# Two stacks of local attention: `weigh` with its operands exchanged, probabilities divided before it, four PSUM banks in one ring, and new orders on all engines

## The reference, cut to what matters

```python
qkv = x @ Wqkv                       # 128 -> 3 x 1024
q = l2norm(q) * qs;  k = l2norm(k) * ksc
q, k = rotary(q), rotary(k)          # per position, with a scale
sim = einsum('bhwie,bhwje->bhwij', bq, bk2) * 8      # 32 queries, 64 keys
attn = softmax(where(mask, -max, sim), -1)
out = einsum('bhwij,bhwje->bhwie', attn, bv2)
x = out @ Wo                         # 1024 -> 128, tokens shifted
hg = layernorm(x) @ W1 + b1          # 128 -> 2 x 341
x = (a * gelu(gate)) @ W2 + b2
```

## Time and profile before

| | us |
|---|---|
| median of 3 runs | 4099.03 (4097.41 to 4099.03) |
| the profiled execution | 4101.54 |
| its span, first to last instruction | 4099.7 |
| PE busy | 3777.4 (92%) |
| DVE busy | 3244.2 (79%) |
| ACT busy | 2461.2 (60%) |
| POOL busy | 2262.3 (55%) |
| from one group's first PE batch to the next one's (731.10 to 800.17) | 69.07 |

### The profile page before, as it was taken

How to read it: one execution, slowest core, us unless ns; L and a number is a source line. 1 busy time by engine, 2 the same in 40 slices (tenths; PEclk the granted TensorE clock), 3 DMA queues, 4 the chain that set the end, 5 groups by cost and what they waited for, 6 DMA issues and landing times. The chain is left out here.

```text
span 4099.7 us, 159711 instructions
## 1 busy us (share of the span) xinstructions
PE 3777.4 (92%) x63216; PEld 2414.3 (59%) x63216; DVE 3244.2 (79%) x11559; ACT 2461.2 (60%) x4393; POOL 2262.3 (55%) x2174
## 2 busy tenths in 40 slices
PE   4689999999999999997699779999999999999997
PEld 2356666666666666663265446666666666666664
DVE  3478888887888888884699778888888788888884
ACT  1257676766767676763522146767676666667674
POOL 1166666666666666662200056666666666666662
PEclk8699999999999999997799789999999999999998
DMA  1032232332322322220000032232232332322221
GB/s 37 27 77 68 74 83 65 78 79 62 78 76 65 87 67 71 71 65 26 0 1 0 6 84 73 65 78 75 72 83 65 79 79 64 79 77 64 76 64 39
DMA packets 170579, 254.11 MB, mean 62 GB/s; under 512 B 36577, under 2 KB 67681, under 8 KB 169697
## 3 DMA queue, kind: packets, MB, share of 16 engines
q1 hardware_dynamic: 169824, 243.74, 23.2%
HBM read 38.08 MB, written 1.05 MB: 10 GB/s over the span
## 5 line engine op out<-in xcount | busy, mean ns | idle before, releaser
L506 PE MATMUL stack_proj<-stack_w_qkv,stack_xs 128*128 128x512 f32 x2304 | 1190.6, 612 | 72.0 <-POOL stack_xs L1137 44.9
L1145 POOL TENSOR_TENSOR stack_roped<-stack_rot_c,stack_rot_s 128x512 f32<-128x512 f32 x768 | 973.7, 1276 | 350.7 <-DVE stack_rot_s L968 350.6
L1155 POOL TENSOR_TENSOR stack_roped<-stack_roped,stack_rnorm 128x512 f32<-128x512 f32 x768 | 813.3, 1070 | 198.7 <-DVE stack_rnorm L1000 198.7
L1163 POOL TENSOR_TENSOR stack_s_m<-stack_s_m,stack_smax 128x512 f32<-128x512 f32 x384 | 402.5, 1048 | 593.7 <-DVE stack_smax L1011 593.6
L966 DVE TENSOR_TENSOR stack_rot_c<-stack_proj,rot_tables 128x512 f32<-128x512 f32 x768 | 527.8, 687 | 229.5 <-PE stack_proj L506 223.7
L1011 DVE CUSTOM_DVE_ANT_0 stack_s_m<-stack_bank_s,band 128x64 f32<-128x64 f32 x3072 | 476.0, 220 | 156.3 <-PE stack_bank_s L529 149.1
L506 PEld LDWEIGHTS stack_proj<-stack_w_qkv,stack_xs 128*128 128x128 f32 x2304 | 369.0, 192 | 307.8 <-issue 138.8
L977 DVE TENSOR_REDUCE stack_ssq<-stack_sq 128x8 f32<-128x512 f32 x768 | 520.5, 678 | 17.5 <-issue 3.5
L805 ACT ACTIVATE stack_sq<-stack_proj 128x512 f32<-128x512 f32 x768 | 460.9, 600 | 109.2 <-DVE stack_rot_s L968 108.5
L968 DVE TENSOR_TENSOR stack_rot_s<-stack_proj,rot_tables 128x512 f32<-128x512 f32 x768 | 521.7, 679 | 0.0
L514 PEld LDWEIGHTS stack_turn<-ident,stack_roped 128*128 128x128 f32 x3072 | 362.6, 141 | 223.9 <-issue 204.0
(11 more groups left out here) (261 smaller groups left out, 5297.1 us busy)
## 6 DMA issues: line engine op xcount, KB each, us to landing
stack_v_w<-stack_v_nat SPq DMA_DIRECT2D x1152, 130.0 KB
stack_v_w<-stack_v_nat SPq DMA_DIRECT2D x768, 65.0 KB
stack_w_qkv<-table_ffn_qkv SPq DMA_DIRECT2D x192, 96.0 KB, 2.4
stack_w_o<-table_ffn_wo SPq DMA_DIRECT2D x12, 512.0 KB, 3.9
stack_w<-table_ffn_w SPq DMA_DIRECT2D x12, 384.0 KB, 3.3
stack_w<-table_ffn_w SPq DMA_DIRECT2D x12, 192.0 KB, 2.9
x_outer<-L_attn_a_X SPq DMA_DIRECT2D x4, 256.0 KB, 3.6
ret_xpos<-table_xpos SPq DMA_DIRECT2D x1, 1024.0 KB, 5.4
```

The lines of the kernel that those rows point to most:

```text
L506: pe.matmul(bank[:, :], xs[:, T, :], w_qkv[:, g.half, col:col + 512], start=True, stop=True).then_inc(done["proj_" + c], 1)
L1145: pool.tensor_tensor(roped[:, i, T % 2, :], rot_c[:, i % 2, :], rot_s[:, i % 2, :], ALU.add).then_inc(done["roped_" + c], 1)
L1155: pool.tensor_tensor(r, r, rnorm[:, T % 2, i, :].unsqueeze(2).broadcast_to([P, 8, HD]), ALU.mult).then_inc(done["united_" + c], 1)
```

## The change

1. `weigh` is turned round: the values (64 rows by 64 columns) are the loaded operand, the probabilities (32 columns) move. It yields the heads transposed, in `bank_o`, from which `heads_out` copies them. `turn_heads` and `norm_heads` are gone, and so is the column of ones, so that the rows that the spread moves are 2,048 instead of 2,080 bytes.
2. The probabilities are divided before that: `sum_probs` and `invert` on DVE, `scale_probs` on POOL, between `exponent` and `turn_probs`.
3. `proj` and `turnb` become one list `work` of four banks, used in turn by everything; `BANK` gives the first index and the row is added to it.
4. New orders on PE, ACT, DVE and POOL. The values are copied at lag 2 instead of 1, the attention after `scores` is at lag 3 instead of 2, `heads_out` half 1 and `mid` at lag 4; `center` moves from T0 of lag 2 to T3 of lag 1. T2 and T3 of PE, cut below, are as T1 but for the MLP: in T2 gate 2 stands where gate 0 is, lin 1 where gate 1 is, nothing where lin 0 is, and lin 2 behind v1; in T3 `center` stands where gate 0 is, `down` between k0 and v1, nothing else of the MLP.
5. SP's waits name `weighed1` and `proj_v1` alone; what it issues, and behind which tile, is unchanged (layer_loads).

```diff
-        proj = [ps("proj0"), ps("proj1")]
-        turnb = [ps("turn0"), ps("turn1")]
+        work = [ps(f"work{n}") for n in range(4)]
...
                     return
-                wait(pe, f"exped{j}", t)
...
                 if not live(t):
                     return
                 wait(pe, f"pt_set{j}", t)
-                if j == 0:
+                if j == FIRST_PV:
                     pe.wait_ge(v_in[T % 2], (2 * g.number + (tile0 // 2 + T // 2 + 1)) * 160)
                 apart(pe, t)
-                for m in range(4):
-                    for gp in range(2):
-                        for n in range(4):
-                            last = pe.matmul(bank_o[WINDOW * n:WINDOW * (n + 1), gp, m * (HD + 1):(m + 1) * (HD + 1)],
-                                             p_t[64 * gp:64 * gp + 64, j, m, WINDOW * n:WINDOW * (n + 1)],
-                                             v_w[64 * gp:64 * gp + 64, T % 2, n, 2 * m + j, :], start=True, stop=True)
+                for half in range(2):
+                    for n in range(4):
+                        for odd in range(2):
+                            for gp in range(2):
+                                m, at = 2 * half + odd, P * half + WINDOW * n
+                                last = pe.matmul(bank_o[HD * odd:HD * (odd + 1), gp, at:at + WINDOW],
+                                                 v_w[64 * gp:64 * gp + 64, T % 2, n, 2 * m + j, :],
+                                                 p_t[64 * gp:64 * gp + 64, j, m, WINDOW * n:WINDOW * (n + 1)],
+                                                 start=True, stop=True)
                 last.then_inc(done[f"weighed{j}"], 1)
-
-            def turn_heads(t, T, g, j, bank):
-                if not live(t):
-                    return
-                wait(pe, f"normed{j}", t)
-                for n in range(4):
-                    last = pe.transpose(bank[:, P * n:P * (n + 1)], o_n[:, j, n // 2, 2 * (n % 2):2 * (n % 2) + 2, :],
-                                        ident[:, :])
-                last.then_inc(done[f"pe_ot{j}"], 1)
...
             def slot(N, T, G, at, of):
+                row = of(0).row
                 if T == 0:
-                    wait(pe, "squared_q1", N - 1)
-                    center(of(2), proj[0])
-                    wait(pe, "v_out0", N - 1)
-                    project_out(*at(3), proj[1])
-                    wait(pe, "ot_set1", N - 3)
-                    variance(of(2), turnb[0])
-                    wait_group(pe, "center_set", G - 2)
-                    project(*at(1), "v1", proj[0])
+                    wait(pe, "kept_q0", N - 2)
+                    project(*at(1), "k1", work[(0 + row) % 4])
                     wait(pe, "kept_k1", N - 2)
-                    turn_probs(*at(2), 0, turnb[1])
-                    wait(pe, "mid_set", N - 3)
-                    project(*at(0), "k0", proj[1])
-                    wait(pe, "v_out1", N - 1)
-                    project(*at(0), "q0", proj[0])
+                    project(*at(2), "v0", work[(1 + row) % 4])
+                    wait(pe, "mid_set", N - 4)
+                    turn(*at(2), "q1", work[(2 + row) % 4])
+                    wait(pe, "kept_k0", N - 2)
+                    project(*at(0), "q0", work[(3 + row) % 4])
+                    wait(pe, "masked1", N - 3)
+                    scores(*at(2), 0)
+                    wait(pe, "squared_k1", N - 1)
+                    turn_probs(*at(3), 0, work[(0 + row) % 4])
+                    scores(*at(2), 1)
+                    wait(pe, "ot_set1", N - 4)
+                    weigh(*at(3), 0)
+                    wait(pe, "v_out0", N - 2)
+                    turn_probs(*at(3), 1, work[(1 + row) % 4])
+                    wait(pe, "kept_q1", N - 2)
+                    project(*at(0), "k0", work[(2 + row) % 4])
+                    wait(pe, "squared_q0", N - 0)
+                    variance(of(2), work[(3 + row) % 4])
+                    wait(pe, "pt_set0", N - 3)
+                    project(*at(2), "v1", work[(0 + row) % 4])
+                    wait(pe, "ot_set0", N - 3)
+                    weigh(*at(3), 1)
+                    wait(pe, "pt_set1", N - 3)
+                    project(*at(0), "q1", work[(1 + row) % 4])
+                    wait(pe, "squared_k0", N - 0)
+                    turn(*at(1), "q0", work[(2 + row) % 4])
                     wait_group(pe, "std_read", G - 2)
-                    turn(*at(1), "k0", turnb[0])
-                    wait(pe, "normed1", N - 3)
-                    weigh(*at(2), 0)
-                    wait(pe, "pt_set0", N - 2)
-                    turn_probs(*at(2), 1, turnb[1])
-                    wait(pe, "kept_k0", N - 1)
-                    turn(*at(1), "q0", turnb[0])
+                    turn(*at(1), "k1", work[(3 + row) % 4])
+                    wait(pe, "v_out1", N - 2)
+                    project_out(*at(3), work[(0 + row) % 4])
+                    wait(pe, "squared_q1", N - 0)
+                    turn(*at(1), "k0", work[(1 + row) % 4])
+                elif T == 1:
...
+                    turn_probs(*at(3), 0, work[(2 + row) % 4])
+                    wait(pe, "v_out0", N - 2)
+                    up(of(2), "gate", 0, work[(3 + row) % 4])
+                    scores(*at(2), 1)
+                    wait(pe, "ot_set1", N - 4)
+                    weigh(*at(3), 0)
+                    wait(pe, "kept_q1", N - 2)
+                    turn_probs(*at(3), 1, work[(0 + row) % 4])
+                    wait(pe, "squared_q0", N - 0)
+                    project(*at(0), "k0", work[(1 + row) % 4])
+                    wait(pe, "pt_set0", N - 3)
+                    up(of(2), "gate", 1, work[(2 + row) % 4])
+                    wait_group(pe, "gelu0", G - 2)
+                    up(of(2), "lin", 0, work[(3 + row) % 4])
+                    wait(pe, "pt_set1", N - 3)
+                    project(*at(2), "v1", work[(0 + row) % 4])
+                    wait(pe, "ot_set0", N - 3)
+                    weigh(*at(3), 1)
...
             def heads_out(t, T, g, j):
                 if not live(t):
                     return
-                wait(act, f"pe_ot{j}", t)
+                wait(act, f"weighed{j}", t)
                 wait(act, "pe_wo", t - 2)
-                act.copy(o_t[:, T % 2, 4 * j:4 * j + 4, :],
-                         turnb[PROJ[f"ot{j}"][T]][:, :].rearrange("p (g n) -> p g n", g=4)
+                act.copy(o_t[:, T % 2, 4 * j:4 * j + 4, :].rearrange("p (g h) n -> p g h n", g=2),
+                         bank_o[:, :, 0:2 * P].rearrange("p g (h n) -> p g h n", h=2)
                          ).then_inc(done[f"ot_set{j}"], 1)
...
             def slot(N, T, G, at, of):
-                heads_out(*at(3), 1)
-                values_out(*at(1), 0)
-                if T == 0:
-                    center_square(of(2))
-                if T == 1 and live_group(G - 2):
-                    act.preload_act_table_set(TABLE)
+                heads_out(*at(4), 1)
                 if T == 2 and live_group(G - 2):
                     act.preload_act_table_set(TABLE)
+                if T == 3 and live_group(G - 2):
+                    act.preload_act_table_set(TABLE)
+                exponent(*at(3), 0)
+                square(*at(1), "q1")
+                keep(*at(2), "q0")
+                keep(*at(2), "k1")
+                keep(*at(2), "k0")
+                exponent(*at(3), 1)
+                if T == 1:
+                    gain_bias(of(2))
+                square(*at(1), "k1")
+                values_out(*at(2), 0)
+                keep(*at(2), "q1")
+                probs_out(*at(3), 0)
                 guess(*at(1))
-                if T == 0:
-                    center_out(of(2))
-                exponent(*at(2), 0)
+                square(*at(0), "q0")
+                if T == 3:
+                    center_square(of(1))
+                if T == 2:
+                    gelu(of(2), 2)
+                if T == 3:
+                    center_out(of(1))
+                if T == 1:
+                    gelu(of(2), 0)
+                probs_out(*at(3), 1)
+                heads_out(*at(3), 0)
                 if T == 0:
                     inv_std(of(2))
-                values_out(*at(1), 1)
-                probs_out(*at(2), 0)
-                exponent(*at(2), 1)
-                keep(*at(1), "k0")
-                if T == 0:
-                    gain_bias(of(2))
                 square(*at(0), "k0")
-                probs_out(*at(2), 1)
-                square(*at(0), "q0")
-                keep(*at(1), "q0")
-                heads_out(*at(2), 0)
-                square(*at(0), "k1")
-                if T == 0:
+                if T == 1:
                     gelu(of(2), 1)
-                keep(*at(1), "q1")
-                if T == 1:
-                    gelu(of(2), 2)
-                keep(*at(1), "k1")
-                square(*at(0), "q1")
-                if T == 0:
-                    gelu(of(2), 0)
```

(90 more changed lines are left out.)

346 lines of the change are left out of this document (149 added, 197 removed), and 2 rows, old and new, of the table NAMES.

## The result

| us | before | after |
|---|---|---|
| median of the runs | 4099.03 | 4369.65 (4357.48 to 4374.49, 4 runs) |
| the profiled execution, its span | 4101.54, 4099.7 | 4370.48, 4368.7 |
| mean of 44 groups, two stacks | 69.3 | 75.4 |

The change makes the kernel slower: ratio 1.0657, 95% interval 1.063 to 1.0684. The forecast was 4323 us in a range of 4110 to 4460. A fourth execution of the kernel before took 4227.10 us in a slower state, and the median leaves it out.

The account below looks back on a forecast made before the run. TensorE (PE) was taken to bound the kernel before. 4101.5 + 77 (values' loop) + 85 (late w_o) + 47 (late MLP weights) + 15 (clock) = 4325.5, median 2.5 lower: 4323 us, range 4110 to 4460.

Parts of the forecast that it names:

- 1 to 3: On PE, heads' turning gone (-3.8 us a group), `weigh` turned round (+1.9), a drain saved (-0.5): 64.5, 66.5 with waits.
- 2, `weigh`: On PE, the 64-column load sets the pace: 1.03 us against 0.79, +0.24 each, +1.9 a group.
- 4, DVE and POOL in a group: DVE's work unchanged, POOL gains two 1.05 us operations a tile, 54 us a group; both lie under PE.
- 5, the loop: Values' copy, spread DMAs, landing, next copy: 70.7 us a group, longer than PE's 64.5; +77 us in all.
- 6, late w_o: Before `project_out` of a layer's first tile, PE stands 9.9 us for w_o; +8.5 a layer, +85 us.
- 7, late MLP weights: On ACT, `gain_bias` waits for vec, queued behind tile 6's spread, and delays v_out0: +4.7 us, ten times, +47.
- 8, clock: PE's clock falls to half after ten stands of 10 us, each losing up to 2.9 us: +15 us.
- item 3: On PE, `scores` half 1 followed at once by `weigh` half 0 saves a drain: -0.5 us a group.
- PE as the bound with late weights: Rival: spread and copy pass in under 9 us, PE stays the bound, late weights cost; 4124 us, chance 0.10.
- The faster case: Rival: PE-bound, layer's late loads half absorbed, `weigh` at most 0.79 us; 3960 us, or 4050 at 1.03; chance 0.09.
- Clock drops in every group: Rival: PE's wait of 3.5 us for v_out0 halves the clock, up to 3 us a group; 4464 us, chance 0.10.
- Dear loads: Rival: loads in `weigh` don't overlap at all, +2.7 us a group on the loop; 4450 us, chance 0.05.

Follow-up runs that it names:

- e4: The changed kernel with w_o's load ahead of tile 1's spread, the MLP's loads ahead of tile 6's, and four v_nat buffers: 3946.05 us, ratio 0.9625.
- e1: The changed kernel with w_o's load issued ahead of the spread of a layer's tile 1 instead of behind it: 4268.64 us, ratio 1.0409.
- e2: The changed kernel with the MLP's loads issued ahead of the spread of tile 6: 4302.1 us, ratio 1.0507.
- e11: e4 with 32 of the 64 columns loaded in each small matmul of `weigh`: 3846.5 us, ratio 0.9396.
- e12: e4 with 16 of the 32 columns moved in each small matmul of `weigh`: 3951.95 us, ratio 0.9643.
- e6: e4 with the row group in `weigh` changing only at every eighth matmul, not at each: 4064.86 us, ratio 0.9907.
- e3: The changed kernel with four v_nat buffers instead of two: 4117.01 us, ratio 1.005.
- e8: The kernel before with four v_nat buffers instead of two: 4100.63 us, ratio 1.0002.
- e5: The changed kernel with only the first five of the ten DMAs of each spread issued: 4027.15 us, ratio 0.9823.
- e9: The changed kernel, two buffers, with the first five DMAs of a spread issued after v_out0 and only the other five waiting for v_out1: 4030.42 us, ratio 0.9825.
- e7: The kernel before with the row group in `weigh` changing at each step instead of every fourth: 4102.93 us, ratio 1.0006.

## Why the prediction was right, point by point

| item | forecast | measured |
|---|---|---|
| 1 to 3, PE's own work a group | 64.5, with waits 66.5 | busy 65.2 in one group of e4; mean of its 44 groups 66.4 |
| 2, `weigh` | 1.03 | 1.065 |
| 4, DVE and POOL in a group | 57.7, 54 | 56.2, 53.8 |
| 5, v_out1 to the end of the next v_out0, four slots | 40.8 | 38.3 (medians into T2, T3, T0, T1: 9.9, 9.0, 9.8, 9.5) |
| 5, v_out0 to v_out1: T1, T2, T3, T0 | 7.7, 6.9, 8.7, 6.6 | 8.0, 6.9, 9.2, 8.0 |
| 5, the loop | 70.7 | 70.3 by these medians |
| 6, late w_o | PE stands 9.9; +8.5 a layer, 85 | 8.7; +9.3 over a quiet group; 101 in e1 |
| 7, late MLP weights | +4.7 a layer, 47 | +5.9; 68 in e2 |
| 8, clock | +15 | some 90 to 110, an estimate (below) |

*Items 1 to 4* held in sum. Of item 3 the sign was wrong: instead of a drain saved, -0.5, the meeting of `scores` and `weigh` brings stands inside the batch, 0.8 us a group in e4 and 1.0 in after. They are in the 66.4 of e4. That so many small instructions in a row outrun their supply is a guess. It fits e11, whose faster `weigh` stands more (66.4 us against 38.4), but no run parted the two batches, and the cause stays open. The load sets `weigh`'s pace (e11, e12), and four share one load's time, as I had taken it. The row that priced it was a 128-column load with 8 moving columns, and halving it gave 0.056 against the 0.058 of the trace. Had I known that this depends on the order of the quarters (e6), it would have been another bound.

*Item 5* held as a mechanism and nearly in size; e3 takes it away, e8 shows that it is new, and e5 and e9 show that what stands behind v_out1 makes it, of which issue is the larger part by the trace. That the sum came out within half a us is partly luck, since two errors offset each other. The issue and landing took 0.3 to 1.2 less a slot than 10.2, 2.5 in all, and the ways from v_out0 to v_out1 2.2 more, 1.4 of it in T0. The prediction let PE's first stand in T0 be the one for v_out0 before `turn_probs` half 1; it comes earlier, at `scores` half 1, which waits for `keep` q1 behind v_out0. In the slot at 691.48 the way then goes over PE as well, since `rotate` k0 waits 0.70 us for PE's k0. Whether rows of 2,048 bytes pass faster than rows of 2,080 no run isolates: the ten issues took 6.6 us (median) in after and 7.1 in before. That the gain of PE would be "all spent in waiting for v_out0" is what e3 shows: with four buffers the quiet groups are 66.2.

*Items 6 and 7* are confirmed by e1 and e2. Removing them gave 101 us for a term of 85 and 68 for one of 47. The clock is part of what is over: groups with a late load spend 10 to 12 us at half, and with the load early 3 to 4.

*Item 8 is the term that was mis-sized.* I let the clock fall in ten stands and counted 15 us. It fell in 46 stretches of the 44 groups, 294 us together, behind the ten late vec and in 14 of the 24 quiet groups as well. A stretch at half speed costs at most half of its length, so 3.1 us cost a quiet group at most 1.6. That is also what lies between the 72.0 that it took and the 70.3 of the loop's medians. (The ten quiet groups in which the clock didn't fall are 69.4 us long; they also waited less, so not all of the 2.6 to 72.0 is the clock.) In the groups with a late load 2.5 to 3.8 us stand over the loop and my terms. Summed, that is an estimate of 90 to 110 us, and half of the 294 us, 147, is the most it can be. No run held the clock while keeping the waits, so the split between wait and clock stays open, and only the sum of both is shown by e1 to e3.

So 4323 against 4370: the loop was put some 20 us too high (70.7 a group, not 70.3, in 47), and the clock some 75 to 95 too low. A miss of 47 us on a loss of 271 is small in part because these two offset each other; 10 to 30 us of the difference stay unaccounted for.

*The rivals.* PE as the bound with late weights (4124) fell, since v_out1 to v_out0 was not under 9 us; e3 measures about that, 4117, once the loop is taken away. The faster case fell. That e4's 3946 lies near its 3960 is chance: it wanted `weigh` at 0.79 and the late loads half won back, and in e4 `weigh` is at 1.065 and the loads are not late. "Clock drops in every group" was partly true: the clock fell in 14 of 24 quiet groups, but only 9 of the 16 falls there have a stand for v_out0, or for `keep` q1 behind it, as the longest just before (6, as that at 992.8, have one inside `weigh`), and they cost at most 1.6 us a quiet group and not 3. Dear loads fell: 1.065, not 1.94.

## What to carry to other kernels

When an order is rearranged for a bound engine, follow each buffer that is filled by DMA once round, from its writer through the issuing queue and the landing back to its writer; if that loop is longer than the bound engine's own work, the gain is lost, and another buffer, or issuing each part of a transfer as soon as its data is there, gives it back. A load that is queued behind a batch of issues is late by the whole batch: put the one with the nearest need first. And count waits of a few us twice, once as waits and once as the lower clock after them; here the second part was an estimated 90 to 110 of the 271 us.

## What the runs showed of the hardware

- Ten DMAs of the spread, issued in a row from one queue, took SP 6.6 us in the median of after (eight of ten times 6.3 to 7.4) and 7.1 in before; five took 3.1 in e5. The median of one was 0.57 to 0.60 us, for 64 KB as for 128 KB, and 0.35 for w_o with 512 KB. The copy that waited for the last one started 1.9 us after its issue ended.
- Sixty-four small matmuls with 32 loaded columns took 0.69 us with 32 moving and 0.79 with 65 moving. With 64 loaded columns they took 1.065 with 32 moving and 1.05 with 16, and 1.385 when eight loads in a row went to two quarters of the array instead of four (e4, e12, e6; 0.69 is e11, 0.79 before and e7).
- Where two batches of 64 small matmuls follow each other at once PE stood for up to 2.2 us (2.7 in e4) inside the second one, with no releaser in the profile, 45 us in all in after (36 stands) and 37 in e4 (46 stands).
- In the 44 groups of after the granted clock was 0.50 in 46 stretches of 3.4 to 10.2 us. The longest stand of PE before one was between 1.3 and 9.8 us. At 0.50 a batch of 16 matmuls took 3.78 us instead of 1.95.
